# One core, a Mamba and experts block on eight images: the scan of an image, the convolution of the next and the experts of the one before, worked in turn behind each scan group

## What is computed

```python
# 1: 32 small convolution paths (1x1 to 4 channels, 3x3, 1x1 to 64), each with norm and relu
x = relu(sum over 32 paths of relu(bn3(w3 . relu(bn2(conv3x3(relu(bn1(w1 . x))))))) + x)
t = x.reshape(8, 3136, 64)
# 2: t = t + core(norm(t)): a Mamba in both directions
#    per direction: xs = silu(conv1d(x @ in_w)); z = x @ in_w2; dt = softplus(xs @ W)
dA  = exp(dt[..., None] * A)                 # 128 channels x 16 states
dBu = dt[..., None] * Bm[:, :, None, :] * xs[..., None]
hs  = scan(a1 * a2, a2 * b1 + b2)            # h[t] = dA[t] * h[t-1] + dBu[t]
y   = (einsum('blds,bls->bld', hs, Cm) + xs * D) * silu(z) @ out_w
# 3: t = t + experts(norm(t)): top 2 of 8 experts, 64 -> 256 -> 64 with gelu;
#    every expert is computed for every token and weighted
```

## Time and profile before

| | us |
|---|---|
| median of 3 runs | 6328.1 (6323.62 to 6338.3) |
| the profiled execution | 6333.79 |
| its span in the trace | 6332.1 |
| image 5 of the loop: convolution | 123.6 |
| projections | 42.7 |
| scan | 406.0 |
| output projection and norm | 50.1 |
| experts, to the next image's first product | 156.9 |

### The profile page before, as it was taken

One profiled execution on the slowest core, in us unless ns is written; L12 is line 12 of the kernel. 1 busy time (PEld: TensorE's weight loads), 2 busy tenths in 40 slices (PEclk: granted clock), 3 DMA queues, 4 the chain that ended last, 5 costly groups with the idle time before them and its releaser, 6 DMA issues. The chain is left out here.

```text
span 6332.1 us, 72725 instructions
## 1 busy us (share of the span) xinstructions
PE 4712.9 (74%) x22126; PEld 1875.5 (30%) x22126; DVE 4177.0 (66%) x6781; ACT 3214.8 (51%) x6875; POOL 3262.2 (52%) x2921
## 2 busy tenths in 40 slices
PE   4766887668876688766977669776797767977669
PEld 2322433214322143221432224322243223332233
DVE  3599635995359944599445994459834699346983
ACT  2555454554545555454554545445454454645545
POOL 1399203992149811498115980159701697017970
PEclk9899788997889988899888998889888998989989
DMA  3356133660335504365033650346413464135631
GB/s 86 82 139 140 26 78 74 147 144 14 88 85 138 135 10 94 79 149 124 18 91 91 139 117 21 87 99 146 102 25 83 108 141 98 28 80 122 140 85 28
DMA packets 205745, 582.54 MB, mean 92 GB/s; under 512 B 75652, under 2 KB 117892, under 8 KB 205188
## 3 DMA queue, kind: packets, MB, share of 16 engines
q1 hardware_dynamic: 205316, 577.47, 39.8%
HBM read 511.20 MB, written 66.20 MB: 91 GB/s over the span
## 5 line engine op out<-in xcount | busy, mean ns | idle before, releaser
L1065 POOL TENSOR_TENSOR hc<-hs,cb 128x448 f32<-128x448 f32 x1792 | 2029.2, 1146 | 329.1 <-DVE hs L1002 329.0
L1002 DVE TENSOR_TENSOR_SCAN hs<-dA,state,ps 128x448 f32<-128x448 f32 x1792 | 2036.4, 1137 | 13.8 <-ACT dA L965 13.8
L991 DVE TENSOR_TENSOR ps<-ps,bb 128x448 f32<-128x448 f32 x1792 | 1095.4, 611 | 309.4 <-PE ps L902 309.1
L952 ACT ACTIVATE state<-hs 128x1 f32<-128x1 f32 x1768 | 357.0, 202 | 1358.0 <-DVE hs L1002 1358.0
L902 PE MATMUL ps<-hx,pick 128*128 128x448 bf16 x2688 | 702.8, 376 | 413.2 <-DVE hs L1002 343.2
L902 PE MATMUL ps<-dux,pick 128*128 128x448 bf16 x2688 | 687.7, 370 | 364.6 <-DVE hs L1002 360.5
L537 POOL TENSOR_TENSOR sp<-hx,dA 128x448 f32<-128x448 f32 x56 | 59.9, 1069 | 1399.2 <-ACT dA L673 1399.2
L1412 DVE SCALAR_TENSOR_TENSOR dA<-ps,be,hs 128x448 f32<-128x448 f32 x224 | 153.2, 684 | 764.2 <-PE ps L1267 677.2
L1346 ACT ACTIVATE rz<-ps,be 128x448 f32<-128x448 f32 x896 | 540.8, 629 | 168.2 <-PE ps L1254 167.1
L1254 PE MATMUL ps<-u,we1s 128*128 128x448 bf16 x2688 | 614.3, 364 | 4.2 <-PEq L1093 4.2
L887 PE MATMUL ps<-hc,gather 128*32 128x448 f32 x3584 | 466.5, 594 | 144.9 <-POOL hc L1065 144.9
(11 more groups left out here) (186 smaller groups left out, 6697.6 us busy)
## 6 DMA issues: line engine op xcount, KB each, us to landing
rz<-dt_scratch SPq DMA_DIRECT2D x112, 896.0 KB, 6.4
x_all<-dt_scratch SPq DMA_DIRECT2D x112, 896.0 KB, 10.0
xn<-dt_scratch SPq DMA_DIRECT2D x112, 896.0 KB, 13.6
dtb<-dt_scratch SPq DMA_DIRECT2D x112, 896.0 KB, 13.3
zs<-h_scratch SPq DMA_DIRECT2D x174, 290.0 KB, 6.0
dt_scratch<-dtx SPq DMA_DIRECT2D x112, 224.0 KB, 1.9
h_scratch<-dA SPq DMA_DIRECT2D x168, 112.0 KB
u<-h_scratch SPq DMA_DIRECT2D x56, 336.0 KB, 4.1
```

The lines of the kernel that those rows point to most:

```text
L952: A.activation(state[:, k % 2, i:i + 1], hs[:, n % RH, at:at + 1], ACT.Copy).then_inc(st_ok, 1)
L991: V.tensor_tensor(bank, bank, bb[:, k % 2, :], ALU.mult).then_inc(bu_ok, 1)
L1002: V.tensor_tensor_scan(rev(hs[:, n % RH, :], d), rev(dA[:, n % RA, :], d), rev(ps[BU[n % 3]][:, 0:CH], d), state[:, d, i:i + 1], ALU.mult, ...
L1065: P.tensor_tensor(hc[:, n % RC, :], hs[:, n % RH, :], cb[:, k % 2, :], ALU.mult).then_inc(hc_ok, 1)
```

## The change

The loop over stages goes. In its place `emit` writes one *round*, a block for all engines of `SLOTS` = 226 slots. With `run` a round scans an image: slot n is group n. With `nxt` it also makes the convolution of the next image, and with `de` the output norm and the experts of the image before. What a slot holds beside its group is fixed by five functions: chunk c has its `third` products in the 11 slots from `conv_at(c)`, its router in those from `tokens_at(c)`, its `up` products in eight of the 16 slots from `expert_at(c)`. The eight images take ten rounds: one with convolution alone, one with scan and convolution, six with all three (three passes of a loop that holds two), one with scan and experts, one with experts alone. All semaphores are cleared between rounds.

PSUM is shared out anew: three banks for groups (`BU`, as before), one for y and the output projection, one (`MISC`) for the step's products and the router's, one for the sums of folds and of `down`, and two in turn (`RING`) for all of `x_T`, `paths_in`, `second`, `third`, `norm_T`, `z`, `up`, `parts` and `pair`: 301 jobs in a full round. A ring job waits until the one two places ahead of it has been read out. Where ACT reads it, this stands a slot later in ACT's order (`up`: in the same slot); where DVE reads it, a slot earlier in DVE's.

Further: `scan(n)` holds both the product with B and the scan of the same group. The decay is made in place in `dtb`, up to `AHEAD` = 6 groups ahead, but not in the slots in which gelu is at work. `u` and `z` are made per step, y is projected per step and added to `res` by DVE (`add_out`). `xn`, the tokens and the input are kept in DRAM and fetched per chunk. The router's choice is made per chunk (25 small DVE operations each, in place of some 26 large ones an image). The sum of the experts' parts moves from DVE to POOL (`add_pair`), the keeping of states from ACT to POOL (`keep_states`, one copy of 128x2 for two groups). The three products that spread dt*u read 32 partitions in place of 128.

```diff
+G = STEPS * DS
...
+RH = 6
+AHEAD = 6
+
+
+def conv_at(c):
+    return 22 + 11 * c
+
+
+def first_at(c):
+    return 2 * c if c < 2 else conv_at(c) - 32
+
+
+def tokens_at(c):
+    return 80 + 16 * c
+
+
+def expert_at(c):
+    return 104 + 16 * c
+
+
+def fold_at(c):
+    return expert_at(c) + (24 if c + 1 < NCH else 21)
...
+SLOTS = G + 2
+DOWN_AT = (4, 7, 12, 15)
+PAIR_AT = (4, 6, 12, 13)
+SUM_AT = (5, 8, 13, 16)
...
+        def emit(p, run, de, nxt, x_img=None, o_img=None):
...
+            A_JOBS = ([(first_at(c), 1, "x_T", c, "act") for c in range(NCH)]
+                      + [(first_at(c) + 2, 1, "paths_in", c, "act") for c in range(NCH)]
+                      + [(conv_at(c) - 11, 1, "second", c, "act") for c in range(NCH)]
+                      + [(conv_at(c) + j * 11 // ZP, 1, "third", (c, j), "act" if j in ACT_J else "dve")
+                         for c in range(NCH) for j in range(ZP)]
+                      + [(conv_at(c) + 22, 1, "norm_T", c, "act") for c in range(NCH)])
+            E_JOBS = ([(expert_at(c) + (m // 2 if m < 8 else 4 + m // 2), 0, "up", c * MT + m, "act")
+                       for c in range(NCH) for m in range(MT)]
+                      + [(tokens_at(c) + 26, 1, "parts", c, "act") for c in range(NCH)]
+                      + [(expert_at(P // PAIRS) + PAIR_AT[P % PAIRS], 2, "pair", P, "act") for P in range(NCH * PAIRS)])
+            RING = sorted((A_JOBS if nxt else []) + (E_JOBS if de else [])
+                          + [(DS * k + 11, 1, "z", k + 1, "act") for k in range(STEPS) if second_half(k)],
+                          key=lambda job: job[0:2])
...
+                    def ring_job(q):
+                        what, of = RING[q][2:4]
+                        if q >= 2:
+                            pe.wait_ge(r_act if RING[q - 2][4] == "act" else r_dve, ring_done[q - 2])
+                        out = ps[RB[q % 2]]
...
+                    def decays_to(n):
+                        while run and decays[0] <= min(n, G - 1):
+                            dA(decays[0])
+                            decays[0] += 1
...
+                        e = n - expert_at(0)
+                        bursting = de and 0 <= e < NCH * DS and e % 8 < 4
+                        silu = k < STEPS and i == 12 and (first_half(k) or second_half(k))
+                        if not bursting and not silu:
+                            decays_to(n + AHEAD)
...
+                        if silu or (de and 0 <= e < NCH * DS and e % DS == 3):
+                            A.preload_act_table_set("natural_log_exp_and_others")
+                        if silu:
+                            decays_to(n + AHEAD)
...
-                    def bu(n):
-                        k, i = n // DS, n % DS
-                        dve.wait_ge(bu_ps, n + 1)
-                        if i == 0:
-                            dve.wait_ge(bcs_ok, 2 * k + 1)
-                        bank = ps[BU[n % 3]][:, 0:CH]
-                        V.tensor_tensor(bank, bank, bb[:, k % 2, :], ALU.mult).then_inc(bu_ok, 1)
...
                     def scan(n):
                         k, i, d = n // DS, n % DS, (n // DS) % 2
-                        dve.wait_ge(bu_ok, n + 1)
+                        bank = ps[BU[n % 3]][:, 0:CH]
+                        dve.wait_ge(bu_ps, n + 1)
+                        if i == 0 and k:
+                            dve.wait_ge(m_act, by_act("bb", k))
+                        V.tensor_tensor(bank, bank, bb[:, k % 2, :], ALU.mult).then_inc(bu_ok, 1)
                         dve.wait_ge(a_ok, n + 1)
                         if n >= RH:
                             dve.wait_ge(hc_ok, n - RH + 1)
-                            dve.wait_ge(st_ok, n - RH + 1)
-                        if n >= 2 * DS:
-                            dve.wait_ge(st_ok, n - 2 * DS + 1)
-                        V.tensor_tensor_scan(rev(hs[:, n % RH, :], d), rev(dA[:, n % RA, :], d),
-                                             rev(ps[BU[n % 3]][:, 0:CH], d), state[:, d, i:i + 1],
-                                             ALU.mult, ALU.add).then_inc(h_ok, 1)
+                            dve.wait_ge(st_ok, (n - RH) // 2 + 1)
+                        dve.wait_ge(bu_ok, n + 1)
+                        V.tensor_tensor_scan(rev(hs[:, n % RH, :], d), rev(dtb[i // 4][:, i % 4, :], d), rev(bank, d),
+                                             state[:, d, i:i + 1], ALU.mult, ALU.add).then_inc(h_ok, 1)
 
...
                         k, i = n // DS, n % DS
-                        if n + 1 < G:
-                            bu(n + 1)
-                        scan(n)
-                        if i == 5 and k:
-                            gate(k - 1)
-                    gate(STEPS - 1)
+                        if run and n < G:
+                            scan(n)
+                            if i == 3 and k:
+                                gate(k - 1)
+                            if i == 6 and k:
+                                add_out(k - 1)
+                        if nxt:
+                            for m in range(len(DVE_J)):
+                                for c in chunk_at(n, lambda c: conv_at(c) + DVE_J[m] * 11 // ZP - 1):
...
+                    def keep_states(n):
                         k, i = n // DS, n % DS
...
+                        at = 0 if k % 2 else CH - 1
+                        P_.tensor_copy(state[:, k % 2, i - 1:i + 1], hs[:, n % RH - 1:n % RH + 1, at]).then_inc(st_ok, 1)
...
+        emit(1, False, False, True, x_img=0)
+        emit(0, True, False, True, x_img=1)
+        with nc.Fori(1, NB - 1, 2) as img:
+            emit(1, True, True, True, x_img=img + 1, o_img=img - 1)
+            emit(0, True, True, True, x_img=img + 2, o_img=img)
+        emit(1, True, True, False, o_img=NB - 2)
+        emit(0, False, True, False, o_img=NB - 1)
```

More of the change, by code:

```diff
@@ new lines, in cut_slab @@
+                    def cut_slab(c):
+                        sp_.wait_ge(h1_out, 16 * min(c + 2, NCH))
+                        if c >= 2:
+                            sp_.wait_ge(r_ps, made("second", c - 2))
+                        for dx in range(3):
+                            at = c * ROWS * PW + dx
+                            sp_.dma_start(slab[32 * dx:32 * dx + 32, c % 2, :, :],
+                                          h1_dram[:, at:at + SLAB].rearrange("(q p) n -> p q n", p=32))\
+                               .then_inc(slab_in[c % 2], 16)
@@ L506, in arrange @@
                         if c >= 2:
-                            sp_.wait_ge(z_ps, ZP * (c - 1))
+                            sp_.wait_ge(r_ps, made("third", (c - 2, ZP - 1)))
                         src = T["h2_scratch"][c % 2].rearrange("a c t n -> (a c) t n")
@@ new lines, in fold_z @@
+                    def fold_z(c, m):
+                        n = len(ACT_J)
+                        if m < n:
+                            src = rz[:, (c * n + m) % 4, :]
+                            pe.wait_ge(r_act, taken("third", (c, ACT_J[m])))
+                        else:
+                            src = acc[:, c % 2, :]
+                            pe.wait_ge(r_dve, taken("third", (c, DVE_J[-1])))
+                        if m == 0 and c:
+                            pe.wait_ge(x1_out, c)
+                        for j in range(KT):
+                            last = MM(ps[AB][0:TT, j * 128:(j + 1) * 128], src[:, j * TT:(j + 1) * TT], ident[:, :],
+                                      is_transpose=True, start=(m == 0 and j == 0), stop=(m == n and j == KT - 1),
+                                      skip_group_check=True)
+                        last.then_inc(z_T, 1)
@@ new lines, in down @@
+                    def down(P):
+                        pe.wait_ge(r_act, taken("up", 4 * P + 3))
+                        if P:
+                            pe.wait_ge(ye_dve, P)
+                        elif nxt:
+                            pe.wait_ge(x1_out, NCH)
+                        for g in range(4 * P, 4 * P + 4):
+                            i = g % 2
+                            last = MM(ps[AB][C * i:C * i + C, 0:CH], we2[:, ORDER[g % MT], :], hg[:, g % 8, :],
+                                      start=(g % 4 < 2), stop=(g % 4 >= 2))
+                        last.then_inc(dn, 1)
@@ new lines, in pair_out @@
+                    def pair_out(P):
+                        c, i = P // PAIRS, P % PAIRS
+                        dve.wait_ge(dn, P + 1)
+                        dve.wait_ge(r_act, taken("pair", P))
+                        if i == 3:
+                            dve.wait_ge(ye_sum, (PAIRS - 1) * c + 1)
+                        out = yw[:, c % 2, :] if i == 0 else yw[:, 2 + i % 2, :]
+                        V.scalar_tensor_tensor(out, ps[AB][:, 0:CH], be2[:, i:i + 1], wb[:, P % 4, :], ALU.add, ALU.mult)\
+                            .then_inc(ye_dve, 1)
@@ new lines, in part @@
+                    def part(kk, a):
+                        x = dux[:, kk % 2]
```

(9 more changed lines are left out.)

1672 lines of the change are left out of this document (732 added, 940 removed).

## The result

The changed kernel takes **6593.4 us** (median of 4 runs, 6549.6 to 6606.4) where the kernel before took 6333.2 beside it: a ratio of 1.040, with a 95% interval of 1.035 to 1.045. It is 4% slower, where 12% faster was forecast. The profiled execution has a span of 6599.0 us.

What follows compares the result with a forecast made beforehand. DVE was taken as the bound: a full round 567 + 59 + 25 + 16 = 667 us, six of them 4002, plus 522, 572, 75, 190, 200 and 2 outside the span, 5563 us; 8 times in 10 between 5080 and 6030.

Steps and rivals of the forecast that it cites:

- The clock: PE in a full round: no stretch of small products alone, so counted at full clock, 544 us of work.
- the falling clock: Rival: ring waits cut PE's work into small pieces, 1.2 GHz is granted, kernel slower than before, 6920 us at 0.65; chance 0.08.
- DVE's other work: DVE in a full round beside scan groups: gate and `add_out` 13 us, convolution 72, experts 99, port waits 59.
- The lost overlap in the scan: DVE's scan group waits for its own product with B: 1.71 us instead of 1.57, 383 us a round.
- The port: DVE operations with two SBUF inputs wait for POOL's `by_c`: 91 a round at 0.65 us, 59 us, bounds 0 and 105.
- The rival that DVE never waits: At the port only POOL waits, as second comer; full rounds 59 us shorter, 5150 us in all; chance 0.22.
- Stalls: 25 and 16 us: Full round: 25 us for waits between engines (bounds 10 and 90), 16 ahead of and behind the round (12 and 30).
- PE is the bound, through the ring: Rival: 301 jobs in two banks wait for read-outs; a round about 715 us, 5850 in all; chance 0.30.
- ACT 428 us a round (422), POOL 445 (451): Work of ACT and POOL in a full round: 422 us and, with copies at 0.2, 451; both under DVE's 626.
- the 70 us that the prediction names as possible on top: ACT: a drain of 1.38 us added to each table load would give 70 us more, still not the bound.
- Preparation and first convolution: Time ahead of the first round with a scan: preparation 75 us, convolution alone 190 (bounds 150 and 280).
- the overlap isn't had: Rival: convolution, experts and scan hold each other up by turns; a round near 750 us, 6200 to 6400; chance 0.05.

Runs made afterwards that it cites:

- e1: The changed kernel with its three picking products per group on all 128 rows again instead of 32: 6211.0 us, ratio 0.980.
- e2: The kernel before the change, with only its picking products cut to the 32 rows that hold something: 7301.5 us, ratio 1.153.
- e4: e1 with POOL's product with C taken over 64 of 448 columns, the other columns left out of the sum: 5986.7 us, ratio 0.946.
- e12: e9 with a ring of three PSUM banks instead of two, and two banks instead of three for the scan's groups: 5963.4 us, ratio 0.942.
- e9: e1 with x fetched ahead of the residual and DVE's SBUF work between product with B and scan, PSUM reads behind the scan: 6052.5 us, ratio 0.955.
- e8: The changed kernel with picking products of 64 rows instead of 32: 6401.0 us, ratio 1.009.

## Why the prediction was wrong, step by step

1. **The clock: the step that failed.** "PE now has no stretch of small products alone, and I count it at full clock" looked at how the work of PE is mixed, and read a product of 32 rows as equal to one of 128, since its columns are the same. At full clock they are (0.20 us from start to start in the changed kernel with 32 rows as in e1 with 128); but with 32 rows the full clock is granted for less of the time. I had named the falling clock as a rival, for a wrong reason (ring waits) and with 0.08. e1 and e2 give its price: 382 us in the changed kernel, 968 in the kernel before. The rival's own arithmetic was too mild as well: it put the break-even at a mean clock of 0.72, and the kernel is slower at 0.763, since it took a round as PE's work divided by the clock plus 16, without any wait. The clock gives the sign of the miss, not the whole of it: e1, at 6211 us, still lies above 6030, my upper bound. Steps 2 to 4 are the terms that were too small by themselves. A full round of e1, counted from start to start, is 407 us of scan groups, 263 of DVE's other work and 82 of waits over 0.2 us; the forecast had 383, 243 and 41.
2. **The lost overlap in the scan.** I put 0.035 us on the wait for the own product, from operations with results in SBUF. The product with B writes PSUM, and there it is 0.13 (0.61 long, 0.74 to the scan). A group takes 1.81, not 1.71, and the groups of a round 24 us more.
3. **The port.** The mechanism was right, in the direction that no row had shown: DVE, coming second, waits. 59 us a round were forecast. e4 takes away 45 with the POOL operation cut to 0.34 us. An estimate of the whole, the sum over DVE's operations besides the scan of what each lasts beyond the shortest of its line and form, gives 80 us for a full round of e1 and 36 for one of e4. DVE's other work takes 263 in e1, with 243 forecast: 20 more. The rival that DVE never waits is out. The Trainium skill (SBUF — State Buffer, section "SBUF: two separate sides") had it so, with the pair held for the whole instruction; e4's 713 and 192 ns agree. The mistake was at the edge: I counted only two-input operations, but casts from SBUF to SBUF wait too, 1.05 instead of 0.18 us (e1, e4).
4. **Stalls: 25 and 16 us.** In e1 DVE's idle time in a full round is 128 us: 30 the own waits of step 2, 13 the short gaps between chained operations, which the forecast's 0.46 already held, and 84 longer waits, 82 on average, against 41 forecast. 33 are waits for picking products (10 of them while PE stands for the first x of the round, whose fetch is behind the load of the residual; I had priced that at nothing), 33 are ahead of the rectifications. This term was the largest miss after the clock, 41 us a round. I had read it off a kernel in which one image at a time is worked, where each queue waits for one thing only.
5. **The ring.** "PE is the bound, through the ring" overstated it: 48 us a round forecast, 15 measured for the third bank (e12, net of the bank that the groups lose), and e9's waits for read-outs, some 50 us, mostly lay under DVE's work.
6. **What held.** ACT 428 us a round (422), POOL 445 (451), the scan's and POOL's durations, the experts alone at about 200 (215 at the end). No drain shows behind the table loads: in the changed kernel the next instruction on ACT starts 1.29 us after the start of a load of 1.28, so the 70 us that the prediction names as possible on top are not there. Preparation and first convolution took 302 instead of 265.

The account of e1 against the forecast: six full rounds of 753 instead of 667 make 516, the first round with a scan 581 instead of 522, the last one with its experts 806 instead of 772, the time ahead 306 instead of 265; together 650. With the clock's 382 this is, but for 2 us, the 1030 by which 6593 missed 5563. That e1 lands at 6211 and 753 a round, where I had put "the overlap isn't had" (0.05), is chance: much overlap is had, DVE being busy 628 of 756 us, but the waits, the port and the slower groups cost what I had given to that rival.

## What to carry to other kernels

Before a product is cut to the rows that hold something, look at the clock row of the stage: the product takes as long with all rows, and the rows that add nothing to the result may be what keeps the engine at its full clock. When two engines share a port, count every SBUF-to-SBUF operation of the one against the long operations of the other, and place them under work that reads PSUM. In an interleaved order, a stall term read from the separate stages can be too small by half, as here; count the lead, in banks, that each in-order queue has over the one that it feeds.

## What the runs showed of the hardware

- PE can be busy all the time and be granted 1.2 GHz: 58.00 of 58.00 us at 0.50 with three of its bf16 products of 32 rows a group; 0.73 with 64 rows at 90% busy (e8), 0.89 with 128 at 79% busy (e1). The Trainium skill (TensorE: Matmul & The Clock Gate, "Part 1: The HAM clock gate") has the clock follow how busy PE has been; measured here, busy time alone does not decide it.
- A DVE operation that waits for its own previous result starts 0.13 us after that result's end when it lies in PSUM (e1: 721.59 and 0.61 to 722.33), 0.03 to 0.04 when in SBUF.
- DVE operations of 0.18 to 0.19 us on 112x32 were recorded at a mean of 0.7 to 1.05 us beside a POOL operation of 1.15; product with B and scan, which read PSUM, kept means of 0.62 and 1.15 (0.61 and 1.14 before).
- A POOL copy of 128x2 takes 0.206 us (changed kernel), where a power on 112x4 takes 1.0.
